# A tensor-product pass over 200,000 sorted edges: its counted ("dense") part grows from 136 to 468 destination nodes, the gathered part shrinks from 42 to 36 rounds

## The reference, cut to what matters

```python
i, j = (edge_index[0], edge_index[1])
summand = _tensor_product(x[i], edge_attr, [w0, w1, w2, w3, w4])     # edge_attr: 9 numbers per edge
out = jax.ops.segment_sum(summand, j, num_segments=x.shape[0])
return out / float(np.sqrt(NUM_NEIGHBORS))
```

## Time and profile before

| | us |
|---|---|
| time, median of 3 runs (7026.89 to 7049.93) | 7041.6 |
| profiled execution, span from its first to its last instruction | 5516.4 |
| median above that span | 1525.2 |
| `tensor_pass` in the span, first gather to last matmul | 1015.4 to 2707.9 |

### The profile page before, as it was taken

One profiled execution on the slowest core, in us unless ns is written; L12 is line 12 of the kernel. 1 busy time (PEld: TensorE's weight loads), 2 busy tenths in 40 slices (PEclk: granted clock), 3 DMA queues, 4 the chain that ended last, 5 costly groups with the idle time before them and its releaser, 6 DMA issues. The chain is left out here.

```text
span 5516.4 us, 98683 instructions
## 1 busy us (share of the span) xinstructions
PE 4206.6 (76%) x27638; PEld 3117.4 (57%) x27833; DVE 2829.6 (51%) x8882; ACT 2333.7 (42%) x5698; POOL 3823.3 (69%) x3904
## 2 busy tenths in 40 slices
PE   3399997477777787777757777778777878579985
PEld 2167665355656666656645555555555555446664
DVE  7898665444444444344365555555555555542225
ACT  2545554222222222222366666666666666331003
POOL 0267776677777777777467777777777777477774
PEclk7599998699999999999878888888888888689997
DMA  1134444222222222222233333333333333165552
GB/s 59 43 134 152 165 155 140 69 58 57 59 58 58 60 58 59 58 59 57 53 76 86 78 86 78 82 82 78 86 78 86 78 85 80 40 215 179 173 173 61
DMA packets 357101, 495.36 MB, mean 90 GB/s; under 512 B 198005, under 2 KB 256838, under 8 KB 345798
## 3 DMA queue, kind: packets, MB, share of 16 engines
q0 software_dynamic: 122368, 254.08, 18.2%
q1 hardware_dynamic: 232046, 237.13, 13.9%
q10 hardware_dynamic: 2400, 0.57, 0.1%
HBM read 400.97 MB, written 90.25 MB: 89 GB/s over the span
## 5 line engine op out<-in xcount | busy, mean ns | idle before, releaser
L3482 POOL DMA_INDIRECT rows_l<-table,idx_l x1568 | 1486.4, 948 | 511.0 <-issue 477.2
L3007 POOL DMA_INDIRECT rows_l<-table,idx_l x1344 | 1270.8, 946 | 432.0 <-issue 409.3
L1645 POOL DMA_INDIRECT rows_l<-table,row_idx x896 | 949.3, 1060 | 301.9 <-issue 271.8
L3039 ACT COPY agg_l<-ps_l 128x288 f32<-128x288 f32 x672 | 268.4, 399 | 1266.3 <-PE ps_l L3217 1252.8
L3217 PE MATMUL ps_l<-hoty_l,rows_l 128*128 128x144 f32 x2688 | 511.3, 315 | 350.9 <-DMA rows_l<-table,idx_l 242.7
L3217 PEld LDWEIGHTS ps_l<-hoty_l,rows_l 128*128 128x128 f32 x2688 | 399.1, 199 | 609.5 <-DMA rows_l<-table,idx_l 394.0
L3702 PE MATMUL p_idle_l<-zeros_l 128*128 128x512 bf16 x1373 | 491.8, 520 | 28.0 <-issue 22.3
L3767 PEld LDWEIGHTS banks_l<-wrow_l,hot_l 128*128 128x128 f32 x3136 | 426.6, 200 | 136.2 <-issue 73.0
L3833 ACT ACTIVATE apart_l<-iota,rel_s_l 128x128 bf16<-128x128 f32 x1568 | 497.2, 387 | 10.1
L3767 PE MATMUL banks_l<-wrow_l,hot_l 128*128 128x136 f32 x3136 | 453.4, 289 | 61.0 <-ACT hot_l L3853 61.0
L3232 PE MATMUL pm_l<-w_mix,agg_l 128*128 128x128 f32 x3024 | 468.7, 285 | 0.4 <-ACT msg_l L3049 0.4
(11 more groups left out here) (607 smaller groups left out, 7581.6 us busy)
## 6 DMA issues: line engine op xcount, KB each, us to landing
eT_l<-in_edges_laid SPq DMA_DIRECT2D x196, 256.0 KB
rows_l<-table,idx_l POOLq DMA_INDIRECT x2912
counts_table<-x_nodes SPq DMA_DIRECT2D x22, 1568.0 KB
x_nodes<-counts_table SPq DMA_DIRECT2D x22, 1568.0 KB
counts_table<-h_nodes SPq DMA_DIRECT2D x21, 1568.0 KB
h_nodes<-counts_table SPq DMA_DIRECT2D x21, 1568.0 KB
rows_l<-table,row_idx POOLq DMA_INDIRECT x896
table<-h_nodes SPq DMA_DIRECT2D x21, 448.0 KB
```

The source lines that it names most:

```text
L1645: pool.indirect_dma_start(out=rows[:, slot, j, :], out_offset=None, in_=table, in_offset=bass.IndirectOffsetOnAxis(ap=what[:, j:j + 1], ax ...
L3007: pool.indirect_dma_start(out=rows[:, u, j, :], out_offset=None, in_=table, in_offset=bass.IndirectOffsetOnAxis(ap=idx[:, u, j:j + 1], axi ...
L3482: pool.indirect_dma_start(out=rows[:, u, j, :], out_offset=None, in_=table, in_offset=bass.IndirectOffsetOnAxis(ap=idx[:, u, j:j + 1], axi ...
```

## The change: what it does

- NODES 136 -> 468, BATCH 17 -> 12 (so 39 batches, and an apply product has 108 columns instead of 153), SKIP 7 -> 13 (so 36 rounds, 144 groups, 576 slots). The caps sum to 781 visits: 253 nodes have one, 172 two, 43 more.
- The one-hots are made for runs of up to 4 visits (`cut_runs`: 190 of 4 and 7 of 3) instead of 2, in a ring of 3 runs.
- Two PSUM banks `pds[m % 2]` take turns over "uses" (a node's visits, an apply, a mix), numbered in program order; `use_taken` counts ACT's copies. To make room for the second bank the gathered part's sums rotate over 3 banks instead of 4. The batch's mix is taken by ACT into `d_out` and added by DVE from there, one group later.
- ACT takes a node in the slot in which it ends, not one later. A batch's mix is placed after the first two tiles of the next batch.
- The plan spreads pieces by weight (visit 3, a node's last visit 5, slice 3, pause 4, mix 2) from slot 20 to the eighth from the end.
- `d_src` and the like become a ring of 127 columns with places by batch; SP may load up to 7 nodes in one group. The mask of a batch is made by one DVE instruction for each stretch of equal caps instead of one for each node.
- `dense_stage` does its row work for 468 nodes (four small matmuls instead of two).
- `d_sums` keeps its layout (written by ACT with a stride of BATCH, read by PE in one run).

```diff
-    NODES, BATCH, SKIP = 136, 17, 7
-    RUN, RING, SLICES, FIRST, TAIL = 2, 6, 7, 32, 12
+    NODES, BATCH, SKIP = 468, 12, 13
+    RUN, RING, SLICES, FIRST, TAIL, LOADS = 4, 3, 7, 20, 8, 7
+    LOADED = 4
...
             for i in mine:
+                if b and i == next(j for j in mine if self.first[j] >= self.columns(b).start + 2):
+                    uses.append(("mix", b - 1))
+                    pieces.append((("mix", b - 1, 0), 2))
+                uses.append(("visit", i))
                 for v in range(self.first[i], self.first[i + 1]):
-                    pieces.append(("visit", i, v))
-            pieces.append(None)
+                    pieces.append((("visit", i, v), 5 if v == self.first[i + 1] - 1 else 3))
+            pieces.append((None, 4))
+            uses.append(("apply", b))
             for k in range(self.SLICES):
-                pieces.append(("apply", b, k))
+                pieces.append((("apply", b, k), 3))
...
+        whole, done = sum(weight for _, weight in pieces), 0
+        for piece, weight in pieces:
             if piece is not None:
-                self.at[self.FIRST + n * room // len(pieces)].append(piece)
+                self.at[self.FIRST + done * room // whole].append(piece)
+            done += weight
...
-        d_hot = sb("d_hot", [P, RING, P])
-        d_row = sb("d_row", [P, RING, Y, A])
+        d_hot = sb("d_hot", [P, RING, RUN, P])
+        d_row = sb("d_row", [P, RING, RUN, Y, A])
-        ps = [bank(f"ps{i}") for i in range(4)]
+        PARTS_HELD = 3
+        ps = [bank(f"ps{i}") for i in range(PARTS_HELD)]
-        pd = bank("pd")
+        pds = [bank(f"pd{i}") for i in range(2)]
...
             def take_dense(w, slot):
-                for kind, n, k in dense.done_before(slot):
+                for kind, n, k in dense.at[slot]:
                     if kind == "visit" and k == dense.first[n + 1] - 1:
+                        m = dense.use_of["visit", n]
                         act.wait_ge(dense_counted, START + w * V + k + 1)
-                        if n >= B:
+                        if n >= B and n % B == 0:
                             act.wait_ge(batch_applied, START + w * dense.batches + dense.batch_of(n))
                         nc.scalar.copy(d_sums[:, :, :, n % B].rearrange("p a c -> p c a"),
-                                       pd[:, 0:wide].rearrange("p (c a) -> p c a", a=A)).then_inc(node_taken, 1)
+                                       pds[m % 2][:, 0:wide].rearrange("p (c a) -> p c a", a=A)).then_inc(use_taken, 1)
...
             def sums(g, q, w):
-                pe.wait_ge(part_taken[q], START + g.k)
+                slot = g.index * PAIRS + q
+                pe.wait_ge(part_taken, START + w * (G * PAIRS) + max(slot + 1 - PARTS_HELD, 0))
...
             def count_visit(w, i, v):
+                r, place = dense.run_of[v]
+                m = dense.use_of["visit", i]
                 if v == dense.first[i]:
-                    if i:
-                        pe.wait_ge(node_taken, START + w * N + i)
-                    if i % B == 0 and dense.batch_of(i):
-                        pe.wait_ge(batch_added, START + w * dense.batches + dense.batch_of(i))
-                if v % RUN == 0:
-                    pe.wait_ge(dense_hot, START + w * (V // RUN) + v // RUN + 1)
+                    pe.wait_ge(use_taken, START + w * USES + max(m - 1, 0))
+                if place == 0:
+                    pe.wait_ge(dense_hot, START + w * RUNS + r + 1)
...
             def apply_batch(w, b, k):
+                m = dense.use_of["apply", b]
                 if k == 0:
-                    pe.wait_ge(node_taken, START + w * N + (b + 1) * B)
+                    pe.wait_ge(use_taken, START + w * USES + m)
...
             def mix_batch(w, b):
-                pe.wait_ge(batch_taken, START + w * dense.batches + b + 1)
+                pe.wait_ge(use_taken, START + w * USES + max(m - 1, dense.use_of["apply", b] + 1))
```

More of the change, by code:

```diff
@@ L1208, in size, with lay_columns @@
     def size(self, b):
-        return self.first[(b + 1) * self.BATCH] - self.first[b * self.BATCH]
-    def room(self):
-        return self.size(0) + self.size(1)
+        return self.columns(b).stop - self.columns(b).start
+    def lay_columns(self):
+        self.room = self.size(0) + self.size(1)
+        self.begin, self.before, at = [], [], 0
+        for b in range(self.batches):
+            if at + self.size(b) > self.room:
+                at = 0
+            over = [c for c in range(b) if self.begin[c] < at + self.size(b) and at < self.begin[c] + self.size(c)]
+            self.begin.append(at)
+            self.before.append(max(over) if over else None)
+            at += self.size(b)
@@ L1238, in plan @@
+        uses.append(("mix", self.batches - 1))
+        pieces += [(None, 4), (("mix", self.batches - 1, 0), 2)]
+        self.uses = len(uses)
+        self.use_of = {use: m for m, use in enumerate(uses)}
         self.groups = (self.sh.rounds - self.SKIP) * U
@@ L1249, in plan @@
         self.adds_at = [[] for _ in range(self.groups)]
+        made_at, begun_at = {}, {}
+        starts = {v: r for r, (v, _) in enumerate(self.runs)}
         for slot, here in enumerate(self.at):
@@ L1315, in _ @@
             pe.wait_ge(row_ready, START + 1)
-            nc.tensor.matmul(p_all[:, 0:N + 2], ones[0:1, 0:P], row[:, :], start=True, stop=True).then_inc(row_spread, 1)
+            for at in range(0, N + 2, 512):
+                end = min(at + 512, N + 2)
+                last = nc.tensor.matmul(p_all[:, at:end], ones[0:1, 0:P], row[0:1, at:end], start=True, stop=True)
+            last.then_inc(row_spread, 1)
         @block.vector
@@ L2844, in tensor_pass @@
         wide = Y * A
-        assert wide <= 512 and Y * B <= 512
+        marks = range(0, seen, P)
+        kinds = sorted(set(dense.caps))
+        assert wide <= 512 and Y * B <= 512 and J * RANGE + P + RUN * A <= 512
         rel = sb("rel", [P, G, J])
@@ L2921, in tensor_pass @@
         shares = ((0, 3), (3, 5), (5, 7), (7, 9))
-        prep_count = 4 * dense.batches + N + dense.batches
+        prep_count = 2 * dense.batches
+        loads_of = [2 * B * DMA * len(range(i, dense.batches, LOADED)) for i in range(LOADED)]
         def count_windows(engine):
@@ L2989, in _ @@
                 sp.wait_ge(idx_loaded[u], START + windows * (R * DMA))
[L2990 to L2991 removed]
+            for i in range(LOADED):
+                sp.wait_ge(dense_loaded[i], START + windows * loads_of[i])
             for i in range(2):
@@ new lines, in prepare @@
+                k = cols.stop - cols.start
+                nc.vector.tensor_scalar(d_part[:, 0:k], d_src[:, cols], P - 1, None, ALU.bitwise_and)
+                for i, n in dense.equal_caps(b):
+                    cap = dense.caps[i]
+                    first = dense.first[i] - dense.columns(b).start
+                    nc.vector.tensor_tensor(d_mask[:, first:first + n * cap].rearrange("p (n k) -> p n k", k=cap),
+                                            d_places[cap][:, :].unsqueeze(1).broadcast_to([P, n, cap]),
+                                            dense.many[:, i:i + n].unsqueeze(2).broadcast_to([P, n, cap]), ALU.is_lt)
```

221 lines of the change are left out of this document (121 added, 100 removed).

## The result

The changed kernel takes 7273.4 us (7251.9 to 7324.4, 4 runs) beside 7034.3 us (7024.5 to 7049.9, 4 runs) of the kernel before: ratio 1.0355, 95% interval 1.0314 to 1.0397, 239 us slower. The forecast had the direction, but 74 us; 7273 lies above its range. Of the later executions of the changed kernel one took 8502.8 us at a granted clock of 0.54; it is in no median or ratio here.

The account below looks back on a forecast made before the run. POOL's gathers bound the pass before; PE, with 1674 us of work, would bound it after. Its end at 2726.7 + 30 hand-overs + 25 clock = 2781.7 against 2707.5, +74 on 7041.6: 7116 us, range 7035 to 7230.

Parts of the forecast that it names:

- What lies around the span: Time of the median outside the profiled span, 1525.2 us, taken as unchanged by the change.
- the gathers' issue sets the time: Tensor-product pass before the change: 1344 gathers 1.250 us apart bound it; PE behind them has 590 us of room.
- Work of PE: PE's priced work in the changed pass: sums and mixing 600, visits 578, applies 420, batch mixes 75, together 1674 us.
- Start of the dense part: First dense piece at slot 20, five groups of 10.0 us after PE's first sums at 1023.5, so at 1073.5.
- Hand-overs and clock: PE's waits for ACT's copies and one-hots, 30 us, plus work lost to half clock after batch mixes, 25 us.
- The room: PE's spare time in the pass before: 1684 us from first sums to last matmul against 1094 of work, 590 us.
- A: The main forecast: PE becomes the bound of the pass, 7116 us, bounds 7061 to 7211; chance 0.62.
- B: PE's apply products cost only their columns, 0.090 us a record, 76 us less: 7040 us, no change; chance 0.12.
- C: POOL's gathers are slower when timed, 1.64 us apart, so POOL stays the bound: 6727 us, faster; chance 0.09.
- D: ACT's copies of single-visit nodes still hold PE up at each, 248 us instead of 30: 7334 us; chance 0.08.
- E: The time outside the span grows with the program's instructions, 7% or 110 us: 7226 us; chance 0.06.
- DVE, priced at nothing: DVE's one-hots and batch preparation in the pass, 1100 us beside 1700 of PE, hidden by being made a group ahead.

Follow-up runs that it names:

- 336 destinations: The changed kernel with 336 dense destinations and 11 skipped rounds instead of 468 and 13; slow chips: 6956, 6956 and 7067 us, ratios 0.9968, 0.9968 and 1.0042 to the kernel before.

## Why the prediction was wrong

**The step that failed** is the last of the sum: "What lies around the span, 1525.2 us in the median, I keep as it is". Nothing lay around it: 2 us in both kernels. By the spans since, the profile was like a quick chip's and the times like slow ones', and the difference sat inside the pass and the passes beside it. With it goes the first step on the chips that were timed, "the gathers' issue sets the time, and PE, in order behind them, has room". On a slow chip POOL waits for PE's sums already before the change. PE starts a group's sums 26 us behind the end of its gathers, where in the first profile it starts 5.5 us ahead of it, and the next gather into that buffer follows 5 us after the sums, where it had 28 us to spare (means over the pass). PE had room there too, as 336 destinations show, but not because it ran ahead of the gathers.

The 264 us of the pass on a slow chip (2435 - 2171) come out in two parts, by the runs without gathers. What PE's own chain takes went from 1263 to 1818 us, +555. What the gathers add to it went from 908 to 617, -291: 192 fewer, and 0.54 instead of 0.68 us each. (On a quick chip they add 433 to the kernel before, by their pace, and 12 to the changed one.) Leaving gathers out is thus worth more there than the 240 us of the forecast, but against the full price of the dense work, not against what overran a room. The shares are differences of runs, not rows. PE's longer busy time, from its lower clock, is a third of each: 1467 - 1150 = 317 of 908, and 1957 - 1743 = 214 of 617. Why a gather adds less in the changed kernel was not tested.

**On a quick chip**, which the argument was about, the mechanism was right and a size was off: +146 us, not +74. From the first gather to the end of the last matmul I had 2781.7 - 1015.4 = 1766 us; it is 1827.

- *Work of PE*, forecast 1674. By distances of consecutive starts in this run (visits 0.371, sums 0.122, the rest 0.112 us): 1562 x 0.371 + 2304 x 0.122 + (2592 + 288 + 3822 + 702) x 0.112 = 579 + 281 + 829 = 1690. Right within 1%; all terms held.
- *Start of the dense part*: 58.1 us after the first gather forecast, 55.9 found. Right.
- *Hand-overs and clock*, forecast 30 + 25. From 1075.8 to 2847.3 are 1771 us, less 1669 of work: 102 us of idling and slow clock. The clock was nearly no part of it: 13.7 us at 1.2 GHz in that stretch, worth 7 (I had 25). Waits for `d_sums`, for which I had 30, are in no row of PE's waits. In their place stands a hand-over that I had not looked at: mixing waits 82 times, 59.2 us, for `msg`. PE, then ACT, on the quick chip:

```profile
1745.74 0.91 PE L3321 MATMUL pd_l<-d_row_l,d_hot_l 128*128 128x441 f32 x2
1746.48 0.65 PE L3285 MATMUL ps_l<-hoty_l,rows_l 128*128 128x144 f32 x4
1747.80 0.94 PE L3299 MATMUL pm_l<-w_mix,agg_l 128*128 128x128 f32 x6 [0.66 <-ACT msg_l L3110]
...
1746.68 0.96 ACT L3078 COPY d_sums_l<-pd_l 128x441 f32<-128x441 f32 x1 [1.20 <-PE pd_l L3321]
1747.43 0.32 ACT L3110 COPY msg_l<-pm_l 128x128 f32<-128x128 f32 x1
```

The copy of a node's sums stands ahead of `msg` in ACT's queue, here and in 81 of the 82 waits. I asked who waits for the new copies and not who stands behind them: with 468 of 0.98 us PE is held 82 times in 144 groups. In the earlier trace rows PE waited for `d_sums`; two banks moved the wait, they didn't remove it. Counted by starts, as the work is, 75 of the 102 us lie between a slot's sums and the mixing behind them, 7 are the clock, and the rest is scattered. No run took the copies out of `msg`'s way, so this share is read from the rows and not tested.

- *The room*: 590 us was too much. PE's chain alone takes 1259 us on a quick chip, not 1094, so the room was 433; 165 us of start, hand-overs and slow clock belong to PE's chain and do not fill up when PE becomes the bound. Setting the 1815 us of the changed chain beside 1692 would have given +123.

One slip of the prediction's own: the upper edge of its range for A, 7211, does not follow from the bounds that it names. Apply records at 0.131 us and the old share of low clock alone give 7116 + 80 + 43 = 7239.

**The signs I named.** Gathers more than 1.4 us apart: 1.56 (1794.5 / 1151) quick, 2.08 slow. Waits for rows gone: 14.8 us from 242.7. Apply starts 0.11 apart: 42 records from 1317.08 to 1321.86,

```profile
1317.08 4.94 PE L3332 MATMUL pd_l<-d_sums_l,h_nodes 128*128 128x108 f32 x42
1321.86 0.43 PE L3285 MATMUL ps_l<-hoty_l,rows_l 128*128 128x144 f32 x2
```

0.114 each. First to last matmul 1758: 1819 quick, 2426 slow.

**The rivals.** B fell with the 0.112. In the Trainium skill, page "TensorE: Matmul & The Clock Gate", the figure of the section "LDWEIGHTS (loading the stationary operand)", 107 ns for 128 columns, is close to it; the 81 ns of the section "Back-to-back issue gap" was not met by these float32 products. C saw that 1525 us were unexplained and that they might be inside the pass, but laid them on the gathers, which are as long as ever; it is the engines beside them that start late while they run. D named 7334 and is near in number, not in kind: PE's waits for `d_sums` are 194 us in 67 waits of up to 5.7 us on the slow chip, and none on the quick one. The copies last 0.97 us on both, so the likelier cause is the late start behind them; that was not separated. E: the time outside the span is 2 us in both kernels. DVE, priced at nothing, stayed hidden (886 us, I had 1100 at most).

## What to carry to other kernels

Set the span beside the timed median before anything else. If they differ by a quarter, the profile may not be of an execution like those that were timed, and the first thing to forecast is which of its waits would grow. Don't add the difference as a constant. A room that a trace shows beside a bound is what the other engine takes alone, hand-overs and all, not the sum of its instructions; when it becomes the bound, ask of each engine's queue what now stands behind the added work. And a wait whose releaser had long been done, on several engines at the same moment, points at a late signal: look for what the moment has in common, and time it by the starts of the engine that waits.

## What the hardware showed that I had not expected

On four of six chips the hand-overs between other engines come late while indirect gathers are queued one behind the other: in the profile of the kernel before, 149 of 430 starts of an idle ACT, by 3.1 us in the median. On the two others none is late (37 ns). That is so in recorded executions, the only ones there are. Of the 1517 us between the span on a slow chip and the first profile's, 479 lie in this pass; without its gathers the kinds differ by 4 us. Another 755 lie where the attention pass gathers, for which that was not tested. Its gathers run from 2775.3 to 4738.2 us in the first profile and, on the slow chip, so:

```profile
L3482 POOL DMA_INDIRECT rows_l<-table,idx_l x1568: 939/946/1333, 3389.8 to 6107.5; - x196
```

With a plain DMA of 0.54 us between two gathers the delay was gone. Whether something useful in its place does the same was not tried.
